# A prefetch of two expert weight sets moved from the down-projection to the start of the next token group (Mamba-2 block and mixture of experts on eight cores)

## The chip, the cores and the metric

The kernel runs on the eight cores of one Trainium2 chip. Each core computes one of eight sequences, with its own copy of the weights, and no core waits for another. The metric is the device time of the slowest core, in microseconds (us). The profile is of one execution, on that core.

## The reference, cut to what matters

```python
x = x + _layernorm(_L0_attn_ref(_layernorm(x), ...))   # Mamba-2 block, 4096 tokens x 1024
# second layer, on h = _layernorm(x):
gate_all = jnp.einsum('nh,ehi->nei', hf, gate_w)       # 8 experts, 1024 -> 512
up_all = jnp.einsum('nh,ehi->nei', hf, up_w)
act = jax.nn.silu(gate_all) * up_all
down_all = jnp.einsum('nei,eih->neh', act, down_w)     # 512 -> 1024, top 4 of 8 by the router
g = jnp.einsum('bsh,hm->bsm', hidden_states, s_gate_w) # shared expert, 1024 -> 2048
u = jnp.einsum('bsh,hm->bsm', hidden_states, s_up_w)
shared = jnp.einsum('bsm,mh->bsh', jax.nn.silu(g) * u, s_down_w)
x = x + _layernorm(routed + shared)
```

## The kernel before, in words

**Two phases.** The first (to about 5,090 us) is the Mamba-2 block, which writes its results `x1_d` and `hb_d` to HBM. The change does not touch it. The second phase (L911 on) is the mixture of experts. It treats the 4096 tokens in eight groups `q` of 512. The shared expert is cut into four pieces of the size of an expert, so a group passes over twelve sets of weights in the order of `pe_order` (L981): the pieces 8 to 11 of the shared expert first, then the experts 0 to 7. A position in this order is called `idx` here.

**One group.** It has these steps.

- The tensor engine waits for `hT`, the transposed activations (L998), and runs 32 small router matmuls (L1002). The vector engine derives the routing weights from them (`router_chain`, L1012).
- For each `idx`, 64 matmuls: 32 with the gate weights `gw` (L1137) and 32 with the up weights `uw` (L1147), the two alternating in blocks of eight. The scalar engine evacuates both, and the vector engine writes the product to `actAll`. Before `idx` 1, four small transposes of the routing weights run (L1107).
- The down-projection, 3 passes of 128 matmuls (L1232), whose weights are in two buffers `de4` of 4 MB each.
- The evacuation: per 128 tokens, layer norm statistics (L311 to L328), the normalized value (L1263), the load of `x1_t` (L1267), the sum (L1271) and the store to `out` (L1275).

**The loads.** `gw` and `uw` have two buffers each, taken in turn (`wb = idx % 2`). `emit_gu_load(pe_i, b)` (L943) issues two DMAs on SyncE's queue (SP), `gw` and `uw`, 1 MB each: L950 and L953 for the shared expert, L945 and L947 for the others. A load for `idx` waits until the tensor engine has done with `idx - 2`. The pieces for `idx` 0 and 1 are the exception. For group 0 they are issued ahead of the loop (L969), for later groups at the start of pass 2 of the group before; `gu_pre` holds the marks of the loads already issued.

**The order on SP.** All DMAs named above, but for the store to `out`, are issued by SP in program order. From pass 0 of one group to the next group, its list is: the `de4` load of the shared weights (L1245, after pass 0), the two early `gw`/`uw` loads, four `x1_t` loads (each after the sum that frees its buffer), `de4` for the next group's pass 0 (L1283), and eight transposing loads of `hT` (L1289).

**Waits on SP's semaphore.** `Prog.wait` has a rule that matters here. Whenever another engine is to wait for a DMA of SP, the wait is for all DMAs that SP has issued so far in program order, and SP itself gets the same wait, once (L81). Behind each such point SP issues nothing until everything ahead of it has landed. A wait of SP for an engine is on L85.

Of the kernel before, what the change touches and what calls it, by code (L numbers as in the profile page):

```python
# [31 lines left out]
EPS_LN = 1e-5  # L32
EPS_RMS = 1e-12
PRE_HT = "evac"
PRE_GU = True
PRE_DE4 = True
TWT_PD7 = False

# [79 lines left out]
def build_core(nc, dbg=(), upto="all", ngroups=NGRP, full_groups=None):  # L118
# [792 lines left out]
    with contextlib.ExitStack() as bstack:  # L911
# [75 lines left out]
        for q in range(ngroups):  # L987
# [200 lines left out]
            for ps_i in range(3):  # L1188
# [17 lines left out]
                elif ps_i == 2:  # L1206
                    p.wait("tensor", "sync")
                    if q + 1 < ngroups and PRE_HT == "down":
                        p.wait("sync", "tensor", hT_guard[1 - hs])
                        for dc in range(8):  # L1210
# [4 lines left out]
                                    transpose=True))  # L1215
                    if q + 1 < ngroups and PRE_GU:
                        p.wait("sync", "tensor", gw_pe_guard[0])
# [149 lines left out]
```

How the kernel before makes its waits and increments, by code:

```python
    def sig(self, eng, fn, inc=1):  # L54
        ch = "gpsimdc" if (eng == "gpsimd" and inc == 1) else eng
        if inc == 1 and eng in ("vector", "scalar", "gpsimd"):
            v = self.cnt[ch]
            if v > 0 and self.last_fence.get(ch + "_self", -1) < v:
                self.thunks[eng].append(
                    (lambda e, s=ch, vv=v: e.wait_ge(self.sem[s], vv), 0, None))
                self.last_fence[ch + "_self"] = v
        self.thunks[eng].append((fn, inc, ch))
        self.cnt[ch] += inc
        return self.cnt[ch]
# [10 lines left out]
    def wait(self, eng, src, val=None):  # L75
        if val is None or src in ("sync", "gpsimd"):
            val = self.cnt[src]
            if src in ("sync", "gpsimd") and src != eng:
                if self.last_fence.get(src, -1) < val:
                    self.thunks[src].append(
                        (lambda e, s=src, v=val: e.wait_ge(self.sem[s], v), 0, None))
                    self.last_fence[src] = val
        if val <= 0:
            return
        self.thunks[eng].append((lambda e, s=src, v=val: e.wait_ge(self.sem[s], v), 0, None))
# [8 lines left out]
                    def body(eng, e=e):  # L94
                        for fn, inc, ch in self.thunks[e]:
                            ins = fn(eng)
                            if inc:
                                ins.then_inc(self.sem[ch], inc)
```

## Time and profile before

| what | us |
|---|---|
| time, median of 2 runs | 7900.83 |
| lowest and highest of them | 7772.51, 8029.15 |
| the profiled execution, device time | 7772.92 |
| its span on the slowest core (core 0) | 7771.3 |
| spans of the eight cores | 7752.7 to 7771.3 |
| second phase, first router matmul to the end | about 2,630 of these |

The span is the time from the first to the last instruction of the core in the profiled execution. Times inside the trace are counted from the span's start. Device time and span of the profiled execution differ by 1.6 us, so a microsecond on the path of the slowest core is read as a microsecond of device time. The profiled execution lies at the lower of the two timed runs.

### The profile page before, as it was taken

How to read it: one execution, taken by the hardware profiler on the slowest of the kernel's cores; microseconds unless marked ns; L12 is line 12 of the kernel's file. 1: busy time of each engine (PE TensorE's matmuls, PEld its weight loads, DVE VectorE, ACT ScalarE, POOL GpSimd, SP SyncE). 2: the span in 40 equal slices, each digit the busy share in tenths (PEclk: the TensorE clock that was granted, in tenths of full speed). 3: DMA queues.
4: the chain of work that ended last, by engine and by line, in shares of the span. 5: the costliest groups of instructions: out<-in, count | busy, mean ns of one | idle time of the engine just before them, and what ended most of it. 6: DMA issues, size and time to landing. Idle time of an engine off the chain costs nothing.

```text
span 7771.3 us, 54102 instructions; the slowest of 8 cores (7752.7 to 7771.3 us)
## 1 busy us (share of the span) xinstructions
PE 3628.4 (47%) x15046; PEld 1420.4 (18%) x15046; DVE 2210.8 (28%) x3625; ACT 1333.0 (17%) x2322; POOL 583.2 (8%) x590
## 2 busy tenths in 40 slices
PE   0033333333333333333332332348778797787977
PEld 0010110110110110110110110123333343333333
DVE  0033243243243243243243243221222112121121
ACT  0011021121121121121121121121212112121121
POOL 1001001001001101101101101100000000000000
PEclk9985565565565565565565565579889898898988
DMA  9921211211211211211211210242332423334331
GB/s 108 115 58 31 49 58 31 49 58 31 49 58 31 52 55 31 55 52 31 55 53 31 56 54 28 56 150 97 136 112 100 144 105 130 114 109 136 114 124 72
DMA packets 401960, 578.63 MB, mean 74 GB/s; under 512 B 227024, under 2 KB 309616, under 8 KB 375424
## 3 DMA queue, kind: packets, MB, share of 16 engines
q1 hardware_dynamic: 325776, 392.59, 16.6%
q0 software_dynamic: 75888, 182.58, 11.4%
q8 instruction: 127, 2.08, 0.1%
q14 instruction: 169, 1.38, 0.1%
HBM read 501.75 MB, written 139.98 MB: 83 GB/s over the span
## 4 chain that ended last, share of the span: by engine, by line
PE 39%; DVE 22%; issue 10%; ACT 9%; DMA 8%; SPq 8%; another core or an unknown queue 3%; DVEq 1%; ACTq 1%; POOL 0%; POOLq 0%
PE PA L1137 9%; PE PB L1147 9%; SPq L830 3%; DVE Mp L717 3%; DVE xdt L245 2%; PE PA L1232 2%; PE PD L1232 2%; PE PC L1232 2%; PE PB L1232 2%; DVE tmp1k L245 2%; ACT es L711 2%; DMA x_d<-x_t 2%; PE PA L546 2%; SPq L1289 2%
## 5 line engine op out<-in xcount | busy, mean ns | idle before, releaser
L476 PE MATMUL PA<-lnuT,W_in_sb 128*128 128x512 bf16 x1152 | 403.4, 517 | 982.2 <-DMA lnuT<-lnu_d 678.3
L1137 PE MATMUL PA<-hT,gw 128*128 128x512 bf16 x3072 | 767.3, 395 | 0.2
L1147 PE MATMUL PB<-hT,uw 128*128 128x512 bf16 x3072 | 737.5, 384 | 0.0
L311 DVE TENSOR_REDUCE stat<-PA 128x1 f32<-128x1024 f32 x16 | 19.6, 1225 | 1320.8 <-PE PD L1232 673.3
L729 PE MATMUL PC<-xdt,Mp 128*128 128x64 bf16 x1024 | 95.3, 233 | 625.2 <-DVE Mp L717 625.2
L717 DVE SCALAR_TENSOR_TENSOR Mp<-es,CBTm 128x512 bf16<-128x512 bf16 x256 | 199.0, 777 | 633.0 <-ACT es L711 633.0
L1147 PEld LDWEIGHTS PB<-hT,uw 128*128 128x128 bf16 x3072 | 304.8, 99 | 377.3 <-issue 26.8
L1137 PEld LDWEIGHTS PA<-hT,gw 128*128 128x128 bf16 x3072 | 302.6, 101 | 387.6 <-issue 61.2
L476 PEld LDWEIGHTS PA<-lnuT,W_in_sb 128*128 128x128 bf16 x1152 | 130.6, 121 | 1251.0 <-issue 1204.5
L1160 ACT ACTIVATE sgs<-PA 128x512 bf16<-128x512 f32 x384 | 229.3, 597 | 673.2 <-PE PA L1137 650.9
L702 PE MATMUL PB<-rhsE,lhsE 66*128 66x512 bf16 x256 | 156.6, 612 | 397.0 <-DVE CBTm L690 397.0
L1170 DVE TENSOR_TENSOR nw_bc<-sgs,sus 128x512 bf16<-128x512 bf16 x256 | 108.9, 425 | 768.2 <-ACT sus L1164 768.2
L711 ACT ACTIVATE es<-PB 128x512 bf16<-128x512 f32 x256 | 152.9, 597 | 994.1 <-PE PB L706 991.2
L1164 ACT ACTIVATE sus<-PB 128x512 bf16<-128x512 f32 x384 | 229.3, 597 | 412.7 <-PE PB L1147 412.3
L546 PE MATMUL PA<-W_in_sb,lnuT 128*128 128x512 bf16 x1024 | 265.7, 406 | 71.9 <-ACT xbc_w L485 36.1
L245 DVE TENSOR_TENSOR xdt<-x_tok,tok64b 128x2048 bf16<-128x2048 bf16 x32 | 179.3, 5602 | 213.6 <-DMA z_sil<-z_d 213.6
L847 PE MATMUL PA<-wout_b,es 128*128 128x512 bf16 x64 | 30.2, 570 | 437.3 <-DMA C_fm<-yb_d 414.7
L729 PEld LDWEIGHTS PC<-xdt,Mp 128*128 128x128 bf16 x1024 | 61.8, 117 | 849.7 <-issue 849.7
L1275 POOL DMA_DIRECT2D out<-out_t x32 | 17.1, 533 | 2657.6 <-DVE out_t L1271 2657.6
L1002 PE MATMUL PD<-rw,hT 128*128 128x8 bf16 x256 | 8.0, 168 | 417.2 <-DMA hT<-hb_d 308.6
L644 PE MATMUL PB<-ident_f,tri64a 64*128 64x64 f32 x32 | 10.7, 335 | 409.6 <-DVE tri64b L640 409.6
L1173 DVE TENSOR_TENSOR actAll<-nw_bc,PC 128x512 bf16<-128x512 bf16 x256 | 176.0, 688 | 27.0 <-DVE nw_bc L1170 0.5
(252 smaller groups left out, 5037.3 us busy)
## 6 DMA issues: line engine op xcount, KB each, us to landing
gw<-gate_bd SPq DMA_DIRECT2D x64, 1024.0 KB
uw<-up_bd SPq DMA_DIRECT2D x64, 1024.0 KB
de<-down_bd SPq DMA_DIRECT2D x36, 1024.0 KB
u_t<-u SPq DMA_DIRECT2D x64, 512.0 KB
wout_b<-W_outT POOLq DMA_DIRECT2D x128, 256.0 KB, 9.7
gw<-sg_bd SPq DMA_DIRECT2D x32, 1024.0 KB
uw<-su_bd SPq DMA_DIRECT2D x32, 1024.0 KB
de<-sd_bd SPq DMA_DIRECT2D x32, 1024.0 KB
```

Source lines behind the costliest of these rows:

```text
L245: return e.tensor_tensor(out.rearrange("q (x y) -> q x y", x=a), in0.rearrange("q (x y) -> q x y", x=a), col.unsqueeze(2).broadcast_to([12 ...
L476: fn = lambda e, f=fc, k=kc, b=bank, gb=gb: e.matmul(b.ap, W_inT[:, k * DPROJ + DIN + f * 128: k * DPROJ + DIN + (f + 1) * 128], lnuT[gb][ ...
L546: p.raw("tensor", lambda e, t=tc, n=ng, k=kc, b=bank, gb=gb: e.matmul(b.ap, lnuT[gb][k][:, t * CH:(t + 1) * CH], W_inT[:, k * DPROJ + n * ...
L711: s_es = p.sig("scalar", lambda e, q=q4, b=bank: e.activation(out=es[q % 2], in_=b.ap, func=AF.Exp))
L717: v_mp = p.sig("vector", lambda e, q=q4: e.scalar_tensor_tensor(Mp[q % 2].rearrange("q (a b) -> q a b", a=4), es[q % 2].rearrange("q (a b) ...
L830: ynT_ld = p.dma("sync", lambda e, f=f8, o=fp * 8, gb=gb: e.dma_start(out=ynT[f], in_=yb_d[gb][:, (o + f) * 128:(o + f + 1) * 128], transp ...
L1137: fn = lambda e, i=ic, k=kc, b=bkg, w=wb, ss=hs: e.matmul(b.ap, gw[w][:, k * 512 + i * 128:k * 512 + (i + 1) * 128], hT[ss][k], start=(k = ...
L1147: fn = lambda e, i=ic, k=kc, b=bku, w=wb, ss=hs: e.matmul(b.ap, uw[w][:, k * 512 + i * 128:k * 512 + (i + 1) * 128], hT[ss][k], start=(k = ...
L1160: s_sg = p.sig("scalar", lambda e, b=bkg, d=slot: e.activation(out=sgs[d], in_=b.ap, func=AF.Silu))
L1164: s_cp = p.sig("scalar", lambda e, b=bku, d=slot: e.activation(out=sus[d], in_=b.ap, func=AF.Copy))
L1173: v_a2 = p.sig("vector", lambda e, k=blk: e.tensor_tensor(actAll[:, k * 512:(k + 1) * 512], scr512b, PC[:, 0:512], OP.mult))
L1232: t=tc, k=blk, f=first, l=last, db=dbuf: e.matmul(b[:, nn * 512:(nn + 1) * 512], actAll[:, k * 512 + t * CH:k * 512 + (t + 1) * CH], de4[d ...
```

## The change

A switch, `PRE_GU`, goes from `True` to `False`:

```diff
-PRE_GU = True
+PRE_GU = False
```

It guards one block, at the start of pass 2 of the down-projection (L1216 on), which is now not emitted:

```python
if q + 1 < ngroups and PRE_GU:
    p.wait("sync", "tensor", gw_pe_guard[0])
    gu_pre[0] = emit_gu_load(8, 0)
    p.wait("sync", "tensor", gw_pe_guard[1])
    gu_pre[1] = emit_gu_load(9, 1)
```

With `gu_pre` empty, the general path in the loop over `idx` is taken for `idx` 0 and 1 of groups 1 to 7 as well:

```python
if idx in gu_pre:
    g_ld = gu_pre.pop(idx)
else:
    p.wait("sync", "tensor", gw_pe_guard[wb])
    g_ld = emit_gu_load(pe_i, wb)
...
p.wait("tensor", "sync", g_ld)
```

Nothing else changes: the same loads into the same buffers, the same matmuls. Group 0 keeps its loads of L969, which `PRE_GU` does not guard.

## Rows read from the trace of the kernel before

**Rows 1.** The waits by line, 5000 to 7771: total us, times, longest.
```profile
PE PD L1002 <- DMA hT<-hb_d: 308.6, 7, 46.0
```

**Rows 2.** Timeline of SP's queue, group 0 to 1: start, us, line, transfer.
```profile
5371.53 3.12 SPq L1245 DMA_DIRECT2D de<-sd_bd  x4
5385.66 0.52 SPq L950 DMA_DIRECT2D gw<-sg_bd  x1
5386.23 0.67 SPq L953 DMA_DIRECT2D uw<-su_bd  x1
5387.00 3.24 SPq L950 DMA_DIRECT2D gw<-sg_bd  x1
5390.28 4.25 SPq L953 DMA_DIRECT2D uw<-su_bd  x1
5394.57 49.01 SPq L1267 DMA_DIRECT2D x_t<-x_d  x4
5448.52 2.79 SPq L1283 DMA_DIRECT2D de<-down_bd  x4
5451.35 19.86 SPq L1289 DMA_TRANSPOSE hT<-hb_d  x8
5490.17 0.53 SPq L950 DMA_DIRECT2D gw<-sg_bd  x1
5490.74 0.67 SPq L953 DMA_DIRECT2D uw<-su_bd  x1
```

**Rows 3.** Timeline of PE over the same boundary: start, us, line, count, idle before.
```profile
5398.92 7.07 PE L1232 MATMUL PA<-de,actAll 128*128 128x512 bf16 x32
5419.64 7.07 PE L1232 MATMUL PD<-de,actAll 128*128 128x512 bf16 x32
5472.75 1.00 PE L1002 MATMUL PD<-rw,hT 128*128 128x8 bf16 x32 [46.04 <-DMA hT<-hb_d]
5473.60 3.57 PE L1137 MATMUL PA<-hT,gw 128*128 128x512 bf16 x8
5476.97 2.75 PE L1147 MATMUL PB<-hT,uw 128*128 128x512 bf16 x8
5479.56 1.89 PE L1137 MATMUL PA<-hT,gw 128*128 128x512 bf16 x8
...
5488.20 1.89 PE L1147 MATMUL PB<-hT,uw 128*128 128x512 bf16 x8
5491.30 0.22 PE L1107 MATMUL PB<-ident_b,w8c 128*8 128x128 bf16 x1 [1.21 <-ACT w8c L1089]
...
5494.31 3.57 PE L1137 MATMUL PA<-hT,gw 128*128 128x512 bf16 x8
```

**Rows 4.** SP's own waits, 5000 to 7771, core 0: total us, times, longest.
```profile
SPq L81 <- DMA uw<-su_bd: 150.2, 17, 10.8
```

**Rows 5.** SP's own waits, 5489 to 5505, core 0.
```profile
SPq L81 <- DMA uw<-su_bd: 7.6, 1, 7.6
```

**Rows 6.** Windows: length, PE, PEld, DVE, ACT, POOL busy, clock, DMA share, GB/s.
```profile
5406.00:5407.00 1.00, 1.00 (x6) 0.49 (x5) 0.00 (x0) 0.00 (x0) 0.00 (x0) 1.00 0.87 348
5410.00:5420.00 10.00, 10.00 (x48) 4.49 (x47) 0.00 (x0) 0.00 (x0) 0.00 (x0) 1.00 0.00 0
5460.00:5470.00 10.00, 0.00 (x0) 0.00 (x0) 1.23 (x1) 0.00 (x0) 0.53 (x1) 0.50 1.05 297
5477.00:5478.00 1.00, 1.00 (x4) 0.43 (x3) 0.69 (x4) 0.63 (x1) 0.00 (x0) 0.50 0.00 0
5478.00:5479.00 1.00, 1.00 (x5) 0.35 (x3) 0.58 (x5) 0.99 (x2) 0.00 (x0) 0.65 0.00 0
```

**Rows 7.** Timeline of the vector engine in the evacuation and the router chain.
```profile
5426.88 1.22 DVE L311 TENSOR_REDUCE stat<-PA 128x1 f32<-128x1024 f32 x1 [83.57 <-PE PD L1232]
5434.39 1.23 DVE L1271 TENSOR_TENSOR out_t<-ffn_ln,x_t 128x1024 f32<-128x1024 f32 x1
5441.94 1.23 DVE L1271 TENSOR_TENSOR out_t<-ffn_ln,x_t 128x1024 f32<-128x1024 f32 x1
5485.23 0.19 DVE L1069 TENSOR_TENSOR w_q<-nw_bc 128x32 f32<-128x32 f32 x1
```

**Rows 8.** SP's own waits, 5000 to 7771, core 5, whose mean is lowest.
```profile
SPq L81 <- DMA uw<-su_bd: 132.8, 17, 11.2
```

## The prediction

> **What bounds the kernel now.** I read the page's slices first. Only the second phase, from about 5,090 us, is touched by the change. Then I took the waits by line of that phase. The tensor engine (PE) waits seven times at the router matmuls of L1002 until the `hT` loads have landed, 308.6 us in all, 44 us at each change of group [rows 1]. Next I laid the timelines of SP's queue and of PE side by side over one such change, from group 0 to 1 [rows 2, 3].
>
> The reader is to see this order. The last down-projection block begins at 5419.64 and ends at about 5426.6. The evacuation follows. SP issues its third and fourth `x1_t` loads when the sums at 5434.39 and 5441.94 are through [rows 7]. Only then, at 5448.52, does SP issue the 4 MB of `de4`, and behind them, from 5451.35, the `hT` transposes. PE resumes at 5472.75. In 5460 to 5470 the DMA engines are full, at 297 GB/s [rows 6]. The boundary is thus bound by SP's serial queue and by the bytes in it. After it, `idx` 0 starts at 5473.60, straight behind the router matmuls, because its weights have been in place since pass 2. From there to the end of the group PE sets the pace, so whatever delays its first gate matmul delays the end by as much.
>
> **What is removed.** In pass 2, four DMAs of 1 MB: SP spends 5385.66 to 5394.54 on issuing them [rows 2]. Who gains? First, PE: four blocks of 32 matmuls start from 5398.92 to 5419.64, so 20.72 / 3 = 6.91 us each, at granted clock 1.00, both while the DMA engines move 348 GB/s and while they move nothing [rows 3, 6]. Their duration does not depend on the transfers. Second, the `x1_t` loads behind them: the first two can be issued some 9 us earlier. But nothing at all is in flight from 5410 to 5420 [rows 6], and the first sum that needs one starts at 5434.39, after the normalization [rows 7]. They were 14 us early already. The third and fourth wait for sums. The `de4` load of pass 2 stands ahead of the prefetch, not behind it. I cost the removal at 0. The cover is those 14 us. Were it gone, it would be worth at most the 9 us of issue.
>
> **What is added.** For `idx` 0, PE now waits for a load that SP can issue only when `hT` has landed, because the wait of L998 also holds SP. The wait for the buffer itself passes at once, since `idx` 10 is long done. I take SP's issue at 5472.75, the moment at which PE is released by the same event. The load takes, by the rows for exactly this pair of transfers (L950, L953):
>
> - issue: 5490.17 to 5490.74 for the first, and 0.67 for the second, with gaps about 1.3 us [rows 2];
> - SP's own wait for the landing: 150.2 / 17 = 8.84 us on this core [rows 4].
>
> Together 10.1 us. Plus 0.1 for PE to start, the gate matmuls begin at 5472.75 + 10.1 + 0.1 = 5482.95 instead of 5473.60: 9.35 us later. From both sides: the shortest wait that I read, 7.6 [rows 5], gives 8.9 for the load and 8.15 for the delay, and the longest, 10.8 [rows 4], gives 12.1 and 11.35. Another core has a mean of 132.8 / 17 = 7.8 [rows 8], so 9.1 and 8.35. I keep the mean of the slowest core.
>
> The Trainium skill's page "DMA: Bandwidth & Descriptors" (section "Anatomy of one DMA") fits 2.0 us plus bytes at 436 GB/s, which for 2.1 MB gives an estimate of 6.8 us; by that the delay would be about 6 us and the sum about 42 us instead of 65. The trace disagrees, with 10.1 us for the pair, and I go by the trace.
>
> **The second load.** The load for `idx` 1 is held on SP until the first has landed (the wait at `idx` 0 is for all of SP's DMAs). It is issued at about 5482.9 and takes another 10.1 us. PE needs it only after `idx` 0 and the four transposes: in the trace from 5473.60 to 5494.31, 20.7 us [rows 3]. It is hidden with 10.6 us to spare. If it took longer than 20.7 us, the rest would be exposed. The load for `idx` 2 waits for the end of `idx` 0 in both versions and keeps its place relative to PE.
>
> **What stands behind the waiting instruction.** On PE, behind the new wait, are all matmuls of the group. The scalar engine's evacuations wait for them and the vector engine's products wait for those. The router chain on the vector engine does not: it runs on behind the router matmuls and ends at 5485.4 as before [rows 7]. Could that earlier end give something back at the transposes? They wait for `w8c` at 5491.30 [rows 3], whose input has been ready since 5485.4. It is in the scalar engine's queue behind the last evacuation of `idx` 0. So nothing comes back.
>
> **The clock.** PE's granted clock is 0.50, that is 1.2 GHz, in the wait and until about 5478.6, and then 2.4 GHz [rows 6]. The first sixteen matmuls therefore take 5479.56 - 5473.60 = 5.96 us where two warm blocks take 3.45: a start costs 2.5 us. It is paid today already, and the start at 5494.31, after a pause of 4 us with four small transposes, looks the same, 3.57 us for the first eight [rows 3]. With the change PE runs 1 us of router matmuls, pauses for 9 us and makes the same start. Between 0 (nothing changes) and 0.4 us (the 0.85 us of router matmuls no longer count toward the rise, at half speed) I take 0.
>
> **The sum.** 7 changes of group (group 0 keeps L969) x 9.35 = 65 us. On the profiled execution: 7773 + 65 = 7838 us, +0.8%. That execution lies at the lower of the two runs shown. Their median is 7900.83, 128 us higher, and the same addition there gives 7966. I forecast against the profiled one.
>
> **The rivals.**
>
> *The load is slowed by its new surroundings (longer, but under 2%).* The load now falls just behind the most loaded stretch of the boundary, and the other cores, which are within 19 us of this one at the end, have theirs around it. At 348 GB/s its 2.1 MB are 6.0 us, so of a load of 8.9 us some 2.9 are fixed. At half the rate it is 12.1 + 2.9 = 15.0 us, a delay of 14.25, and x 7 = 100: 7873. For it: the wait ranges from 7.6 to 10.8 by chance already [rows 4, 5]. Against it: the same neighbours surround the load of `idx` 2 now, and it is fast.
>
> *Slower by over 2%: the second load is exposed as well.* With L the time of a load, the delay is L - 0.75, plus L - 20.7 where L exceeds 20.7. 2% is 155 us, 22.2 per change, which needs L = 21.8: under a third of the rate, at all seven. At L = 22 it is 22.55 x 7 = 158: 7931. Nothing in the rows comes near: the longest load is 12.1.
>
> *Not slower: the delay is absorbed.* This needs a place behind the first gate matmul where PE waits for something that does not move with it. The only one that I can name is the router chain before `idx` 1, and its result lies ready 5.5 us before it is read. Or the 9 us of issue in pass 2 bring something forward. Both are excluded by the rows above as far as I see. The time would be 7773. That the switch does nothing is excluded too: the block of L1216 is its only use.
>
> **How the numbers follow.** Exposed once, as worked out: 0.80, 7838. Slowed load: 0.10, 7873. Not slower or gaining: 0.05, 7773. Second load exposed: 0.05, 7931. For the range, the low end is the bare transfer, 6.0 us without anything fixed: 5.25 x 7 = 37, 7810. The high end is the forecast on the median of the timed runs, 7966, since the timed runs of the kernel before lie 256 us apart and that spread is larger than the uncertainty of my sum; it takes in the two slower rivals. The likeliest case's own range is 7830 (8.15 us each) to 7852 (11.35 each). About 2% is what a measurement of this kernel can tell from no change. Under it lie the forecast, the slowed load and the third rival: within 2% 0.91, slower 0.06, faster 0.03.
>
> **What the changed profile would show.** SP's timeline: no L950 or L953 at 5385, `x1_t` loads from about 5386, and a pair L950, L953 within 0.2 us of the last `hT` landing, the next pair 10 us later. PE: a wait for `uw` between L1002 and L1137, seven times, 9 us each, where now there is none; none at `idx` 1. The down-projection blocks still 6.91 us, the wait at L1002 still 44 us, the first eight gate matmuls still about 3.4 us. I would be wrong if the wait at L1002 shrank by several us (then pass 2 or the boundary had been disturbed by the prefetch), if the new wait were 14 us or more, or if `idx` 1 waited too.

## The result

| what | before | after |
|---|---|---|
| time, median of all runs, us | 8029.54 (10 runs) | 7866.84 (11 runs) |
| lowest of them | 7770.56 | 7846.02 |
| ratio after / before | | 1.0103, 95% interval 1.0086 to 1.012 |
| profiled execution, device time | 7772.92 | 7852.82 |
| its span, slowest core | 7771.3 (core 0) | 7851.3 (core 6) |

In many executions the cores of one die run at a lower granted clock for part of the time, which lengthens them by up to 6%, whatever the kernel, so the ratio and the comparisons below leave such executions and cores out, and the medians of all runs can't be compared. The change costs 1.0%, 80 us. The forecast was 65 us.

The waits by line of the changed kernel, core 6 (total us, times, longest), of PE and then of SP's own queue:

```profile
PE PD L1002 <- DMA hT<-hb_d: 318.8, 7, 46.8
PE PA L1137 <- DMA uw<-su_bd: 24.1, 2, 12.1
PE PA L1137 <- DVE w_q L1069: 22.9, 2, 11.5
PE PA L1137 <- DVE nw_bc L1044: 17.5, 2, 9.0
PE PA L1137 <- DVE nw_bc L1058: 9.8, 1, 9.8
...
SPq L81 <- DMA uw<-su_bd: 278.1, 31, 12.3
```

The first row answers [rows 1]. The four rows of L1137 are new. They are seven waits, 74.3 us in all, ahead of the first gate matmul. Only two of the seven are put down to the transfer. The other five name a router operation of the vector engine that happens to end about then; no instruction of PE waits for those, and the weights are what it waits for. SP's timeline shows that.

The timelines of SP and of PE of the same core over the change from group 0 to 1:

```profile
5379.62 58.62 SPq L1267 DMA_DIRECT2D x_t<-x_d  x4
5443.46 2.87 SPq L1283 DMA_DIRECT2D de<-down_bd  x4
5446.68 19.48 SPq L1289 DMA_TRANSPOSE hT<-hb_d  x8
5468.04 0.54 SPq L950 DMA_DIRECT2D gw<-sg_bd  x1
5468.62 0.67 SPq L953 DMA_DIRECT2D uw<-su_bd  x1
5477.94 0.52 SPq L950 DMA_DIRECT2D gw<-sg_bd  x1
5478.50 0.67 SPq L953 DMA_DIRECT2D uw<-su_bd  x1
5494.84 0.52 SPq L950 DMA_DIRECT2D gw<-sg_bd  x1
...
5468.06 0.99 PE L1002 MATMUL PD<-rw,hT 128*128 128x8 bf16 x32 [46.74 <-DMA hT<-hb_d]
5478.07 3.57 PE L1137 MATMUL PA<-hT,gw 128*128 128x512 bf16 x8 [9.01 <-DVE nw_bc L1044]
5481.43 2.96 PE L1147 MATMUL PB<-hT,uw 128*128 128x512 bf16 x8
5484.23 1.89 PE L1137 MATMUL PA<-hT,gw 128*128 128x512 bf16 x8
...
5495.97 0.22 PE L1107 MATMUL PB<-ident_b,w8c 128*8 128x128 bf16 x1 [1.21 <-ACT w8c L1089]
```

The order is the forecast one. The first pair is issued when `hT` has landed (5468.04, PE starts at 5468.06), the second when the first has landed (5477.94), and PE begins with `gw` 0.13 us behind that. Where [rows 2, 3] had 0.85 us between the router and the first gate matmul, there are now 10.01.

The distance between the two issues is the time of the first load. Over the seven changes of group on this core it is 9.9, 13.0, 9.4, 12.6, 12.9, 10.7 and 12.4 us: 11.55 on average, where the sum had 10.1.

### The profile page after: what moved, and what is told of

Its sections match the earlier page's. It is cut to its first block, busy times and chain, and to the rows that moved or that the text cites. A ratio compares the mean times of both kernels' runs of the same rounds, so it can differ in the third digit from the quotient of the medians.

```text
span 7851.3 us, 54116 instructions; the slowest of 8 cores (7826.6 to 7851.3 us)
## 1 busy us (share of the span) xinstructions
PE 3627.6 (46%) x15046; PEld 1420.8 (18%) x15046; DVE 2210.6 (28%) x3625; ACT 1333.0 (17%) x2322; POOL 582.3 (7%) x590
## 4 chain that ended last, share of the span: by engine, by line
PE 38%; DVE 22%; issue 10%; ACT 9%; DMA 8%; SPq 8%; another core or an unknown queue 3%; DVEq 1%; ACTq 1%; POOL 0%; POOLq 0%
PE PA L1137 9%; PE PB L1147 9%; SPq L830 3%; DVE Mp L717 3%; DVE xdt L245 2%; PE PA L1232 2%; PE PD L1232 2%; PE PC L1232 2%; PE PB L1232 2%; DVE tmp1k L245 2%; ACT es L711 2%; DMA x_d<-x_t 2%; PE PA L546 2%; SPq L1289 2%
## 5 line engine op out<-in xcount | busy, mean ns | idle before, releaser
L1137 PE MATMUL PA<-hT,gw 128*128 128x512 bf16 x3072 | 765.7, 394 | 74.6 <-DMA uw<-su_bd 24.1
L1137 PEld LDWEIGHTS PA<-hT,gw 128*128 128x128 bf16 x3072 | 302.4, 100 | 462.1 <-issue 135.8
L1002 PE MATMUL PD<-rw,hT 128*128 128x8 bf16 x256 | 7.9, 168 | 423.5 <-DMA hT<-hb_d 318.8
L644 PE MATMUL PB<-ident_f,tri64a 64*128 64x64 f32 x32 | 10.7, 336 | 409.5 <-DVE tri64b L640 409.5
L1232 PE MATMUL PA<-de,actAll 128*128 128x512 bf16 x768 | 175.8, 388 | 20.0 <-DVE actAll L1173 20.0
```

The costliest lines, as they stand in the source:

```text
L1137: fn = lambda e, i=ic, k=kc, b=bkg, w=wb, ss=hs: e.matmul(b.ap, gw[w][:, k * 512 + i * 128:k * 512 + (i + 1) * 128], hT[ss][k], start=(k = ...
L1232: t=tc, k=blk, f=first, l=last, db=dbuf: e.matmul(b[:, nn * 512:(nn + 1) * 512], actAll[:, k * 512 + t * CH:k * 512 + (t + 1) * CH], de4[d ...
```

## Where the 80 us are

I split the spans of the two slowest cores at the first router matmul.

| | before, core 0 | after, core 6 | difference |
|---|---|---|---|
| span, us | 7771.3 | 7851.3 | +80.0 |
| up to the first router matmul | 5141.8 | 5135.8 | -6.0 |
| second phase | 2629.5 | 2715.5 | +86.0 |
| first gate matmul, beyond the 0.85 us behind the router | 0 | 75.4 | +75.4 |
| waits for `hT` at L1002 | 308.6 | 318.8 | +10.2 |
| seven first positions, gate matmul to transposes | 120.5 | 122.3 | +1.8 |

The first phase is the same code, and its end differs between the cores of one execution (5115.8 to 5141.8 before), so the -6.0 is spread and not effect. The last three rows add up to 87.4; the missing -1.4 is spread over the rest of the group. The +10.2 is mostly a difference between cores too: over all eight cores the waits for `hT` are 312.9 before and 314.5 after. The delay is not. Over the eight cores it is 74.5 on average (68.7 to 82.4), 10.65 us at each change of group. The first position takes 17.1 us before and 17.5 after.

The second phase by itself, without the spread of the first, is 81.8 us longer on the average of the eight cores (2713.3 against 2631.5). The waits for `hT` give 1.6 of it, the delays 74.5, the first positions 2.7, and the rest of the group about 3.

So the place, the count and the mechanism were right, and one term was too small: 10.65 us instead of 9.35. The experiments ask why a load that took 10.1 us at `idx` 2 and 3 takes 11.5 us here.

## What the trace says about the load's length

A load of this core is slow when its neighbour moves data. To see this I compare windows of two cores. The profile has no common clock for them, and the times of each are counted from its own first instruction, so that windows with the same numbers are simultaneous is an assumption. The rates support it to about a microsecond: in the changed kernel the rate of a core within its loads is most opposed to that of its partner when the partner's times are shifted by 0.25 to 1.0 us, on all eight cores.

These are one-microsecond windows of the changed kernel (length, busy times, clock, DMA share, GB/s), first of core 6, then of core 7:

```profile
5811.00:5812.00 1.00, 0.00 (x0) 0.00 (x0) 0.64 (x4) 0.00 (x0) 0.00 (x0) 0.50 0.78 154
5814.00:5815.00 1.00, 0.00 (x0) 0.00 (x0) 0.68 (x4) 0.00 (x0) 0.00 (x0) 0.50 0.93 282
6153.00:6154.00 1.00, 0.00 (x0) 0.00 (x0) 0.65 (x4) 0.00 (x0) 0.00 (x0) 0.50 1.05 361
```

```profile
5811.00:5812.00 1.00, 1.00 (x6) 0.49 (x5) 0.00 (x0) 0.99 (x2) 0.00 (x0) 1.00 1.06 362
5814.00:5815.00 1.00, 1.00 (x6) 0.49 (x5) 0.00 (x0) 0.57 (x1) 0.00 (x0) 1.00 0.15 52
6153.00:6154.00 1.00, 1.00 (x4) 0.37 (x3) 0.54 (x3) 0.00 (x0) 0.00 (x0) 0.50 0.00 0
```

At 5811 core 6 is in its late load (the one of 13.0 us) and gets 154 GB/s, while core 7 gets 362. What core 7 is loading there is its second late pair, the one for `idx` 1: its PE is already at work on `idx` 0. When that pair is nearly through, at 5814, core 6 rises to 282. At 6153 core 7 moves nothing, core 6 gets 361, and that load is the one of 9.4 us. The DMA engines of core 6 are busy for 0.78 of the slow window, so they are not idle, their packets take longer.

The split is not by the core's number but by who came first. Core 7 had issued that pair 0.8 us ahead of core 6 (5806.2 against 5807.0). Cores 0 and 1 at 5796, where core 0 had issued its second late pair 1.8 us ahead of core 1's first (5790.7 against 5792.5):

```profile
5796.00:5797.00 1.00, 1.00 (x4) 0.33 (x3) 0.00 (x0) 0.49 (x1) 0.00 (x0) 0.60 1.09 369
5796.00:5797.00 1.00, 0.00 (x0) 0.00 (x0) 0.58 (x5) 0.00 (x0) 0.00 (x0) 0.50 0.87 169
```

In the windows of all eight cores around 5810 and 6150 I find the same in 2 and 3 and in 4 and 5: the later one is at 110 to 260 GB/s until the earlier one is through, and the earlier one is at 330 to 380. It holds for the whole second phase of the changed kernel. There are 140 times at which both cores of a pair are loading weights and one has issued at least 0.5 us ahead; the earlier one is the faster in 139 of them. With less than 0.5 us between the issues, which is within the doubt about the alignment, it is the faster in 27 of 41.

How much the later one loses goes with what is loaded. In the 38 of these cases in which both load weights of the shared expert, the earlier core has 355 GB/s and the later one 129 on average. In the 89 in which both load weights of the other experts, it is 405 and 282. The tile of another expert lies in one piece of HBM, that of the shared expert is cut out of a larger array, in rows of 1 KB (L952). One of the 89, core 0 and then core 1, which had issued 2.4 us ahead:

```profile
5890.00:5891.00 1.00, 1.00 (x6) 0.48 (x5) 0.00 (x0) 0.00 (x0) 0.00 (x0) 1.00 0.83 319
5890.00:5891.00 1.00, 1.00 (x6) 0.45 (x5) 0.00 (x0) 0.06 (x1) 0.00 (x0) 1.00 0.97 410
```

That the layout is the reason is not shown: no run changes it, or puts another expert first.

In the trace of before, too, the core that reaches its first router matmul later than its partner waits longer for the shared weights, in all four pairs: 8.8 us on average against 7.9 (cores 0 and 1), 8.2 against 7.9, 8.4 against 7.8 and 8.4 against 7.9. In all four it is also the one with the even number, so this alone does not tell the two apart. Over all 56 first late loads of the changed kernel I set the length against the bytes that another core moved from 1 to 9 us behind the issue. The correlation is 0.65 for the pair's other core and 0.36 or less for every other pairing. The experiments below are the better test.

The Trainium skill's page "HBM Reference" (section "Specifications (TRN2)") says that two cores share a memory domain and that with both streaming each gets about 358 GB/s. The trace agrees on the sharing between two cores, not on the halves: 154 and 362 here, together 516, and the earlier load keeps its full rate. Two loads of the other experts come to 687 together.

## The experiments

My theory, A: the delay is the time of the first late load, less 0.85 us, one for one. The load is a fixed part plus bytes, and bytes are slower while the partner core moves its own. The rivals: B, both late loads cost; C, the loss comes from lost overlap elsewhere; D, a load behind the `hT` loads is slow in itself.

I give delays per change of group as read from PE's timeline (first gate matmul less first router matmul less 0.85 us), averaged over the seven changes and over the cores, all eight or those named. Times are compared with those of before on the same chip.

### Only idx 0 late

```diff
     if q + 1 < ngroups and PRE_GU:
-        p.wait("sync", "tensor", gw_pe_guard[0])
-        gu_pre[0] = emit_gu_load(8, 0)
         p.wait("sync", "tensor", gw_pe_guard[1])
         gu_pre[1] = emit_gu_load(9, 1)
```

> Only the weights of idx 0 are loaded late, behind the hT loads; those of idx 1 are prefetched in pass 2 as before. Theory A (only the first late load is exposed, and it is slowed by what the partner core moves at that time): PE waits for uw between L1002 and L1137 seven times, 9.3 to 10.8 us each, a little shorter than in the changed kernel since one of the two late pairs is gone from every core's boundary; time +65 to +75 us on before. Theory B (both late loads cost): about half the loss, +40 us. Theory C (the loss is not the load but lost overlap elsewhere): the wait at L1002 changes by several us.

Measured: 7851.3 (one run), against 7773 to 7786 for before: about +72. The delay is 9.0 us (cores 4 to 7) instead of 10.65, a little under what I expected. It is 9.7 on cores 4 and 6, which are 8 us ahead of their partners and load beside the partner's `de4` and `hT`, and 8.3 on cores 5 and 7, whose partners are through by then. Theory B falls: with one of two late loads gone the loss is nearly whole. The shorter load fits A: one of each partner's two late pairs is gone from the stretch in question. The wait at L1002 is 45 us, as before, so C has nothing to stand on. A delay shorter by 12 us in all hardly shows in the time of the slowest core, but it does in the second phase by itself, which is 2702.4 us on these cores where the changed kernel has 2713.3. So the second late pair, which costs its own core nothing, lengthens its partner's first, by 1.65 us per change as these two runs compare and by 1.4 as the run without loads for `idx` 1 to 3 has it.

### Only idx 1 late

```diff
     if q + 1 < ngroups and PRE_GU:
         p.wait("sync", "tensor", gw_pe_guard[0])
         gu_pre[0] = emit_gu_load(8, 0)
-        p.wait("sync", "tensor", gw_pe_guard[1])
-        gu_pre[1] = emit_gu_load(9, 1)
```

> Only the weights of idx 1 are loaded late; those of idx 0 are prefetched in pass 2. Theory A: the load is issued when hT has landed and has some 20 us until PE needs it, so nothing waits: within 10 us of before, no wait at idx 0 or idx 1. Theory B (both late loads cost): +40 us.

Measured: 7777.4 (one run), level with before. The delay is 0 on all cores (0.1 us at most on average). SP's timeline of core 2, the slowest, and the transposes that close `idx` 0:

```profile
5468.65 0.54 SPq L950 DMA_DIRECT2D gw<-sg_bd  x1
5469.22 0.67 SPq L953 DMA_DIRECT2D uw<-su_bd  x1
5485.45 0.52 SPq L950 DMA_DIRECT2D gw<-sg_bd  x1
...
5486.59 0.22 PE L1107 MATMUL PB<-ident_b,w8c 128*8 128x128 bf16 x1 [1.22 <-ACT w8c L1089]
```

The pair of 5468.65 has 18 us until the transposes start. A load of 10 to 13 us hides there: the second half of the change is free.

### The late pair issued with the hT loads

```diff
             if PRE_HT == "evac" and q + 1 < ngroups:
                 ...                         # eight transposing loads of hT
+                gu_pre[0] = emit_gu_load(8, 0)
```

This is the changed kernel with the pair for `idx` 0 directly behind the transposes, so SP does not wait between them, and PE waits for both together at L1002.

> The pair for idx 0 is issued directly behind the hT transposes, with no wait of SP between; the pair for idx 1 stays late as in the changed kernel. Theory A: the fixed part of the load (issue and landing, about 3 us) now lies under the hT loads, and what is left is the transfer of 2.1 MB at 300 to 370 GB/s: the wait at L1002 grows by 6 to 8 us instead of a separate wait of 10.8, time +42 to +56 us on before. Rival: the load is bound by the chip's memory and not by latency, so nothing is gained against the changed kernel, +80 us.

Measured: 7849.2 (one run), about +70. The wait at L1002 (core 0; in the profile it stands with the eighth, the start of group 0):

```profile
PE PD L1002 <- DMA uw<-su_bd: 494.6, 8, 107.0
```

Seven of the eight are 387.6, and over all cores the mean is 379.0 against 312.9 before: +9.4 us each (9.0 on cores 0, 1, 6 and 7 alone), not 6 to 8. Against the changed kernel's 10.65 only 1.2 to 1.6 us are hidden. My expectation missed. The next run puts the fixed part of a load at 2.85 us; why no more of it was hidden here is not shown.

### Half the bytes late

```diff
     if q + 1 < ngroups and PRE_GU:
         p.wait("sync", "tensor", gw_pe_guard[0])
-        gu_pre[0] = emit_gu_load(8, 0)
-        p.wait("sync", "tensor", gw_pe_guard[1])
-        gu_pre[1] = emit_gu_load(9, 1)
+        emit_gu_load(8, 0, "uw")            # only uw
...
-                    g_ld = emit_gu_load(pe_i, wb)
+                    g_ld = emit_gu_load(pe_i, wb, "gw" if idx == 0 else "")
```

`emit_gu_load` gets a third argument for this, which names the one part to load (not printed here).

> Of the pair for idx 0, uw is prefetched in pass 2 and only gw (1 MB) is loaded late; the pair for idx 1 is late as in the changed kernel. Theory A (the delay is a fixed part of about 3 us plus bytes over a rate shared with the partner core): delay of the first gate matmul about half of what the bytes cost, 3 + 3 to 5 = 6 to 8 us less the 0.9 of the router: 5.5 to 7 us instead of 10.7. If latency dominated it would stay above 8.

Measured: 6.3 us (cores 0 to 3), between 5.0 and 8.3 for single ones. The shortest of 1 MB is 5.0 and the shortest of 2 MB, in the run with only `idx` 0 late, is 8.0. The second megabyte costs 3.0 us, which for 1.05 MB is 350 GB/s, near the rate of the windows with a quiet partner. So I estimate a lone load of this pair at 5.0 + 0.85 - 3.0 = 2.85 us of fixed part and 3.0 for each MB, 8.85 in all. What lies above, 2.7 us in the changed kernel's average of 11.5, I put down to the other core; the run with only `idx` 0 late and the one without loads for `idx` 1 to 3 bear this out, where cores with a quiet partner come down to 8.0 to 8.3.

### The late pair twice

```diff
                 p.wait("sync", "tensor", gw_pe_guard[wb])
                 g_ld = emit_gu_load(pe_i, wb)
+                if q > 0 and idx == 0:
+                    p.wait("sync", "sync")
+                    g_ld = emit_gu_load(pe_i, wb)
```

> The changed kernel with the late pair for idx 0 of groups 1 to 7 loaded twice, the second time after the first has landed. Theory A: whatever the load takes comes out of PE one for one, so the delay rises from 10.7 to about 21 to 23 us at each change of group, about 75 us more than the changed kernel in all. If other work covered part of it, the rise would be smaller.

Measured: 20.6 us (cores 0, 1 and 4 to 7) where one load gave 10.65, and the second phase of these cores is 75 us longer than the changed kernel's, as expected. The first change on core 4:

```profile
5482.52 3.57 PE L1140 MATMUL PA<-hT,gw 128*128 128x512 bf16 x8 [21.30 <-DMA uw<-su_bd]
```

What the load takes comes out of PE, and no part of it is covered.

### No loads for idx 1 to 3

```diff
-                    p.wait("sync", "tensor", gw_pe_guard[wb])
-                    g_ld = emit_gu_load(pe_i, wb)
+                    if q == 0 or idx not in (1, 2, 3):
+                        p.wait("sync", "tensor", gw_pe_guard[wb])
+                        g_ld = emit_gu_load(pe_i, wb)
```

> The changed kernel without the loads for idx 1, 2 and 3 of groups 1 to 7 (PE computes these with what lies in the buffers, so that part of the result is left out). It takes away most of what the other cores move while this core loads its first pair. Theory A (contention with the partner): the first load falls from 11.5 to about 9.5 to 10.3 us, delay 8.7 to 9.5. Rival (a load behind the hT loads is slow in itself): it stays at 11.5.

Measured: 9.3 us (cores 2 to 5; 9.1 over all eight) instead of 10.65. Rival D falls, since the load behind `hT` is as it was. The four cores are not alike, though: 11.1, 8.3, 8.7 and 9.1. Core 3 was 26 us behind its partner in this execution, so core 2's late load (issued at 5816.0) fell on core 3's last `x1_t`, its `de4` and its `hT` loads. Router and first gate matmul of cores 2 and 3 at the same change, and a window of each:

```profile
5816.03 1.00 PE L1002 MATMUL PD<-rw,hT 128*128 128x8 bf16 x32 [42.09 <-DMA hT<-hb_d]
5827.04 3.57 PE L1138 MATMUL PA<-hT,gw 128*128 128x512 bf16 x8 [10.01 <-DVE nw_bc L1060]
5819.00:5820.00 1.00, 0.00 (x0) 0.00 (x0) 0.64 (x4) 0.00 (x0) 0.00 (x0) 0.50 0.89 214
```

```profile
5842.15 1.00 PE L1002 MATMUL PD<-rw,hT 128*128 128x8 bf16 x32 [42.93 <-DMA hT<-hb_d]
5851.00 3.57 PE L1138 MATMUL PA<-hT,gw 128*128 128x512 bf16 x8 [7.86 <-DVE nw_bc L1049]
5819.00:5820.00 1.00, 0.00 (x0) 0.00 (x0) 0.32 (x2) 0.26 (x1) 0.00 (x0) 0.50 0.98 401
```

Core 3, whose partner had no load left to do, is at 8.0 us, the figure of the lone load. Core 2, beside a partner at 401 GB/s, is at 10.2.

### The change without the de4 load at the boundary

```diff
-            if PRE_DE4 and q + 1 < ngroups:
-                p.wait("sync", "tensor", pe_down_last)
-                ...                         # four loads of 1 MB, de4 of the next group
...
                     g_ld = emit_gu_load(pe_i, wb)
+                if q > 0 and 5 <= idx < 9:
+                    j_ = idx - 5
+                    p.wait("sync", "tensor", act_pe_guard)
+                    g_ld = p.dma("sync", lambda e, j=j_: e.dma_start(
+                        out=de4[0][:, j * 4 * DM:(j + 1) * 4 * DM], in_=down_bd[j]))
```

> The changed kernel, with the de4 load of the next group taken out of the boundary (1 MB each beside the weights of idx 5 to 8 instead). The hT transposes and the late pairs stay at the boundary. Theory A: hT alone lands some 9 us earlier, and the partner core too moves 4 MB less there, so the first late load meets less of it: wait at L1002 about 36 us instead of 45, delay of the gate matmul 8.5 to 9.5 instead of 10.7. In all about 75 us less than the changed kernel, level with before within 20 us. Rival: the pause is set by the evacuation or the transposes, the wait at L1002 stays above 42.

Measured: 7799.7 and 7810.8 against 7787.3 for before, so about +18, and some 60 us less than the change alone. The second phase by itself is 3.6 us longer than before on the average of the cores; the slowest core, 4, is late at the end of the first phase (5152.9) and longer than the others in the second (2656). The wait at L1002 is 33.6 us (36 expected) instead of 44.9. The delay is 10.2 instead of 8.5 to 9.5: a miss. Taking the partner's `de4` away helps the late load little. That the two cores of a pair are still within reach of each other's late loads fits this, but no run shows it by itself.

### A version that beats both: hT in pass 2

Before, with `PRE_HT = "down"` (the `hT` loads at the start of pass 2, ahead of the prefetch) and the `de4` edit above.

> The prefetch of idx 0 and 1 stays in pass 2, the hT transposes go there too, ahead of it, and the de4 load of the next group leaves the boundary: 1 MB each beside the weights of idx 5 to 8 of the group. Theory: the boundary is bound by SP's queue and its bytes, so PE's pause shrinks from 46 us to what the evacuation needs (last normalized value at about 31 us behind the last matmul): 15 us less, seven times, -105 us on before. Rival: the 1 MB pieces lengthen the loads of idx 5 to 8 from 9 to 12 or 13 us, near the 13.8 to 16.7 us of cover, and the transposes delay the x1 loads in pass 2; then half of it or more is given back.

Measured: 7669.0 to 7677.5 in four runs, ratio to before 0.9862, interval 0.9845 to 0.9879: 1.4% faster. The wait at L1002 on core 5, the slowest:

```profile
PE PD L1002 <- DVE ffn_ln L1268: 214.3, 7, 30.8
```

30.6 us each instead of 44, and it ends with the last normalized value of the evacuation and no longer with a transfer. Over all cores the seven waits are 214.5 against 312.9: 98 us come from there. The pieces beside `idx` 5 to 8 make no wait.

### The change applied to that version

```diff
-PRE_GU = True
+PRE_GU = False
```

> v1 (hT in pass 2, de4 beside idx 5 to 8) with the change under study applied: PRE_GU False. Now SP has nothing left at the boundary but the x1 loads, the last of which lands about 9 us ahead of the end of the evacuation, so the late load for idx 0 can run under the evacuation. Theory A (what the change costs is the missing cover behind the hT loads, nothing else): delay of the first gate matmul 0 to 2 us instead of 10.7, time within 15 us of v1, about 7675. Rival: a late load costs its 10 us wherever it is put: 7745.

Measured: 7703.0 and 7708.8, 81 us under before on the same chip (7787.3), where v1 was 107 under its own. The delay is 1.7 us instead of 10.65. On core 2, the slowest, and with the longest delays, SP and PE run like this:

```profile
5447.08 0.53 SPq L950 DMA_DIRECT2D gw<-sg_bd  x1
5447.66 0.67 SPq L953 DMA_DIRECT2D uw<-su_bd  x1
5458.81 0.52 SPq L950 DMA_DIRECT2D gw<-sg_bd  x1
...
5456.03 1.00 PE L1002 MATMUL PD<-rw,hT 128*128 128x8 bf16 x32 [31.40 <-DVE ffn_ln L1268]
5459.31 3.19 PE L1142 MATMUL PA<-hT,gw 128*128 128x512 bf16 x7 [2.29 <-DMA uw<-su_bd]
```

The same late load, 11.7 us here, starts at 5447.08, 9 us ahead of the router matmuls, under the evacuation. The same edit that costs 80 us behind the `hT` loads costs about 25 here: 26 by these times, on two chips, and 24.6 by the second phases alone (2550.7 against 2526.1). The delays of the gate matmul are 12 of it, the first positions 3, the waits at L1002 1.5, and about 8 are spread over `idx` 1 to 11 and not explained. My 15 us were too few, the rival's 70 far too many.

### The evacuation in another order

v1, with `for n_, tc in enumerate([3, 0, 1, 2])` in the evacuation, and with PE waiting at the change of group for the loads up to the first `x1_t` load only.

> v1 with the evacuation in the order PD, PA, PB, PC, and with PE waiting at the change of group only for the loads up to the first x1 load instead of for all. The router matmuls can then start after the first evacuation (about 8 us behind the last matmul instead of 31) and the first gate block after the second. The scalar engine's own evacuations of idx 0 stand behind the group's evacuation in its queue, so PE can run at most 4 blocks of eight ahead. Theory: 7 to 12 us less at each change of group than v1, seven times: 50 to 85 us, to about 7600. Rival: PE runs its four blocks at the low clock, pauses, and starts again at the low clock, so that hardly 5 us are gained.

Measured: 7680.0 (one run), no better than v1. The rival had the size right: hardly anything is gained. PE and the scalar engine of core 3 over one change:

```profile
5478.70 1.00 PE L1011 MATMUL PD<-rw,hT 128*128 128x8 bf16 x32 [7.83 <-DVE ffn_ln L1280]
5486.15 3.36 PE L1154 MATMUL PA<-hT,gw 128*128 128x512 bf16 x8 [6.45 <-DVE ffn_ln L1280]
5493.70 3.57 PE L1164 MATMUL PB<-hT,uw 128*128 128x512 bf16 x8 [4.20 <-DVE ffn_ln L1280]
...
5506.69 3.32 PE L1154 MATMUL PA<-hT,gw 128*128 128x512 bf16 x8 [4.86 <-ACT sgs L1177]
...
5505.95 0.60 ACT L1177 ACTIVATE sgs<-PA 128x512 bf16<-128x512 f32 x1
```

PE starts 23 us earlier, but then waits 6.45, 4.20 and 4.86 us, and each start is at the low clock (3.3 to 3.6 us for a block of eight instead of 1.73). The first two waits are for banks that the evacuation of the group still holds. The third is for the scalar engine: its first evacuation of `idx` 0 comes at 5505.95, behind the group's own evacuation and the router's exponential. Of the 22.8 us, 6.6 are given back before the first gate matmul and 14.2 in `idx` 0 (31.1 us instead of 16.8). How much of these 14.2 is the clock and how much the queue of the scalar engine was not tested.

## Why the prediction was wrong

**The direction of the number.** The sum said slower, by 65 us on the profiled execution of 7773. But the number on record, 7838, lies below the median of the two runs shown, 7900.83, and the range reached on both sides of it, so as a time beside the given one it reads as a gain. The measured effect, +1.0% with an interval clear of 1, is a loss. The step that failed is the last of the part on the sum, "I forecast against the profiled one": I took one execution as the base and did not say what sign that leaves against the other base. The base itself was right: the three shortest executions of before are 7770.6, 7772.5 and 7787.1, and the 7900.83 is the mean of one of these and one of 8029.15. Likewise the high end of the range, 7966, is the forecast on that median and no limit of the effect. A forecast of an effect should be read off a ratio, here 1.008.

**The size.** The failing term is "SP's own wait for the landing, 150.2 / 17 = 8.84". It was measured at `idx` 2 and 3, and I carried it to the boundary. There it is 10.3 on the slowest core of after (11.55 less 1.25 of issue). The runs showed in its place a lone load of 8.85 us in all, and on top of it 2.7 us of the partner core's transfers. The rival of the slowed load named the mechanism, with the neighbours' traffic, and priced it at 14.25 us of delay with a chance of 0.10; the truth, 10.65, lies between forecast and rival. The excess is 1.3 us x 7 = 9 us. I had the hint in hand: 7.6 to 10.8 by chance, and two cores apart, 7.8 and 8.8 [rows 4, 5, 8]. That the likeliest case's own range, 8.15 to 11.35 us, holds the measured 10.65 is in part luck: its upper end is the longest single wait, taken seven times, and not worked out from what slows a load.

The fit quoted from the Trainium skill, page "DMA: Bandwidth & Descriptors", is given there, in the section "Anatomy of one DMA — SWDGE (gpsimd) path", for DMAs that GpSimd issues. The loads here are issued by SP, so the 10.1 us of the trace do not contradict the page.

**What is removed.** Right. The blocks of the down-projection still take 6.91 us, and the wait at L1002 is 44.9 us over all cores against 44.7.

**The second load.** Right for its own core, and shown by the run with only `idx` 1 late. What the part on it left out is the partner: with the second pair prefetched the first load's delay falls from 10.65 to 9.0 us.

**The clock.** I took 0 and gave 0.4 as the upper bound. The first position is longer by 0.4 us over all cores, 3 us in all, and all of it lies in the first sixteen matmuls (5.83 us against 5.45). But the reason that the prediction gave for its upper bound, router matmuls that no longer count, does not hold up: with only `gw` late (a pause of 6 us) these take 5.43 us, and with the pair loaded twice (a pause of 20 us) 5.51. Where the 0.4 comes from stays open.

**The absorbed delay.** Excluded rightly for this kernel: the load made twice costs twice. It becomes real when the boundary has slack on SP, as in the change applied to v1.

**The rest.** From 65 to the 82 us of the second phase, as an average over the cores: 9 from the load, 3 from the first positions, 2 from the waits for `hT`, and 3 in the rest of the group, which I can't place.

## What to carry to other kernels

A prefetch is worth what its place covers. Here half of it (`idx` 1) was worth nothing by itself, since the general path had 18 us of cover, and the other half its full duration. With both late, the loss is about 1.5 us more per change, through the partner core. Ask for each load separately when the queue can issue it, what that queue waits for by then, and when the first reader comes. A queue that is held until everything ahead has landed turns each late load into latency plus bytes, so the gain lay in emptying the boundary (1.4%) and not in the prefetch that was there. When a load's price is taken from another place of the trace, look at what the partner core moves there and here.

## What the runs showed of the hardware that I had not expected

- Two neighbouring cores (0 and 1, 2 and 3, 4 and 5, 6 and 7) slow each other's loads, and not evenly: the one that issued 0.8 us earlier got 362 GB/s and the later one 154; alone a core reaches 361. The earlier one was the faster in 139 of 140 cases of the changed kernel. Two loads of shared weights ran at 355 and 129 GB/s on average, two of the other experts at 405 and 282.
- A pair of 1 MB loads of shared weights, beside a quiet partner, takes 8.85 us, by my estimate from two runs 2.85 us plus 3.0 us for each MB; in the changed kernel it takes 9.4 to 13.0 us on core 6.
- A router burst of 1 us, 9 us of pause and then dense matmuls start at the same low clock, 3.57 us for the first eight, as after 46 us of pause.
